# A fused routing, self-attention and cross-attention layer: the projections of each query chunk moved into the routing loop, and the last chunk's end split in two

## The reference

```python
# layer 0: routing, each 128 rows of x against all 1601 context rows
tok = input_tokens @ W_proj + b_proj
attn = softmax(prev_states @ tok.T / sqrt(D)); routed = attn @ tok
ps_n, in_n = _ln(prev_states), _ln(routed)
u, r = sigmoid([ps_n, in_n] @ W_u + b_u), sigmoid([ps_n, in_n] @ W_r + b_r)
cand = tanh([r * ps_n, in_n] @ W_n + b_n)
x = _ln((1 - u) * prev_states + u * cand)
# layer 1: 16 heads of 16
x = x + _mha(_ln(x), _ln(x), sa...)     # self-attention, 2048 keys
x = x + _mha(_ln(x), context, ca...)    # cross-attention, 1601 keys
x = x + gelu(_ln(x) @ w1.T + b1) @ w2.T + b2   # 1024 hidden
```

## Time and profile before

| what | value |
|---|---|
| median of 3 runs | 1587.95 us (1584.9 to 1590.18) |
| profiled execution | 1583.61 us, span 1581.9 us |
| PE busy | 1472.7 us, 93% of the span |
| ACT busy | 1068.4 us, 68% |
| DVE busy | 536.6 us, 34% |
| POOL busy | 43.9 us, 3% |

### The profile page before, as it was taken

How to read it: one execution, slowest core, us unless ns; L and a number is a source line. 1 busy time by engine, 2 the same in 40 slices (tenths; PEclk the granted TensorE clock), 3 DMA queues, 4 the chain that set the end, 5 groups by cost and what they waited for, 6 DMA issues and landing times.

```text
span 1581.9 us, 21204 instructions
## 1 busy us (share of the span) xinstructions
PE 1472.7 (93%) x8062; PEld 636.8 (40%) x8062; DVE 536.6 (34%) x1286; ACT 1068.4 (68%) x1285; POOL 43.9 (3%) x62
## 2 busy tenths in 40 slices
PE   8889999998787999999999999899899999999967
PEld 5467777776332222322322322222223432432334
DVE  2435555556532022232330431232332232143140
ACT  2323333332345999999999999789788787797731
POOL 2100000000110000000000000000000000000000
PEclk9999999999897999999999999899999999999988
DMA  7300000000397000010010254501000000000000
GB/s 233 153 7 7 7 7 7 7 3 0 82 245 135 18 15 11 11 49 11 12 39 22 33 94 71 113 34 34 15 19 14 22 11 11 21 15 1 8 7 14
DMA packets 37672, 64.07 MB, mean 41 GB/s; under 512 B 6164, under 2 KB 21844, under 8 KB 37428
## 3 DMA queue, kind: packets, MB, share of 16 engines
q1 hardware_dynamic: 32024, 40.87, 12.3%
q0 software_dynamic: 5552, 21.89, 3.8%
HBM read 40.85 MB, written 22.02 MB: 40 GB/s over the span
## 4 chain that ended last, share of the span: by engine, by line
PE 74%; ACT 16%; DVE 4%; issue 3%; DMA 2%; DVEq 0%; SPq 0%; ACTq 0%; POOL 0%; POOLq 0%
PE PS L962 22%; PE PS L945 16%; ACT PX L680 14%; PE PS L759 6%; PE PS L768 6%; PE PS L1019 5%; PE PS L1031 4%; PE PS L1002 2%; PE PS L805 2%; PE PS L731 2%; PE PS L706 2%; PE PS L735 1%; PE PS L777 1%; PE PS L780 1%; PE PS L981 1%
## 5 line engine op out<-in xcount | busy, mean ns | idle before, releaser
L680 ACT ACTIVATE PX<-PS 128x1024 f32<-128x1024 f32 (+1 forms) x928 | 883.9, 1039 | 144.7 <-PE PS L945 93.8
L962 PE MATMUL PS<-PX,V 128*32 128x512 f32 (+1 forms) x3712 | 500.3, 611 | 5.0 <-ACT PX L680 3.0
L945 PE MATMUL PS<-QST,stack 50*128 50x512 f32 (+1 forms) x1856 | 386.0, 473 | 24.8 <-DMA QST<-shift 10.6
L945 PEld LDWEIGHTS PS<-QST,stack 50*128 50x128 f32 (+1 forms) x1856 | 156.2, 186 | 427.4 <-ACT PX L680 341.3
L962 PEld LDWEIGHTS PS<-PX,V 128*32 128x32 f32 (+1 forms) x3712 | 73.7, 108 | 152.4 <-issue 127.1
L1381 DVE COPY OT<-PS 128x512 f32<-128x512 f32 x32 | 22.1, 692 | 302.0 <-PE PS L962 300.7
L607 ACT ACTIVATE PR<-PS,small 128x1601 f32<-128x1601 f32 x16 | 25.6, 1597 | 107.2 <-DVE small L1218 107.2
L759 PE MATMUL PS<-tokF,XT 128*128 128x512 f32 (+1 forms) x256 | 95.1, 525 | 0.6 <-DVE small L1150 0.6
L768 PE MATMUL PS<-tokT,PT 128*128 128x256 f32 (+1 forms) x416 | 93.3, 381 | 0.6 <-DVE CZ L1267 0.6
L768 PEld LDWEIGHTS PS<-tokT,PT 128*128 128x128 f32 (+1 forms) x416 | 77.9, 190 | 10.7 <-issue 0.8
L1031 PE MATMUL PS<-W,HIDT 128*128 128x256 f32 x256 | 65.2, 404 | 10.6 <-ACT HIDT L666 9.8
(11 more groups left out here) (134 smaller groups left out, 1168.4 us busy)
## 6 DMA issues: line engine op xcount, KB each, us to landing
QST<-q_parts SPq DMA_DIRECT2D x192, 64.0 KB
q_parts<-PARTS POOLq DMA_DIRECT2D x16, 512.0 KB, 5.3
stack<-k_parts SPq DMA_DIRECT2D x24, 256.0 KB, 10.1
stack<-k_parts SPq DMA_DIRECT2D x24, 200.1 KB, 6.8
k_parts<-KPARTS POOLq DMA_DIRECT2D x8, 512.0 KB, 12.6
v_cross<-V POOLq DMA_DIRECT2D x1, 3328.0 KB, 10.0
V<-v_cross SPq DMA_DIRECT2D x2, 1664.0 KB, 13.2
k_parts<-PARTS POOLq DMA_DIRECT2D x6, 512.0 KB, 3.4
```

What stands on the lines that cost most here:

```text
L680: act.activation(PX[0:kr, (2 * t + half) % 4, :, :], PS[0:kr, slot:slot + 2, :], ACT.Exp, scale=SCALE).then_inc(at["exp"], 1)
L945: ins = pe.matmul(PS[0:kr, 2 * (n % LOOK) + jj, :], KST[a][lo:lo + NROW, pair, kt * P:kt * P + kr].bitcast(F32R), QST[lo:lo + NROW, pair, ...
L962: ins = pe.matmul(PS[32 * j:32 * j + 32, 6, :], V[0:kr, kt, 2 * (g // 2 * GH + j) + g % 2, :], PX[0:kr, (2 * t + j // 2) % 4, j % 2, :], s ...
```

## The change

The routing loop is written out turn by turn on all engines. Stage 3 is cut into its four chunks. Chunk 0 comes as a whole after turn 7, chunk 1 after turn 11, chunk 3 after turn 19 (`DENSE`), and chunk 2 is put inside turns 16 and 17 (`WITHIN`), the first six entries in turn 16. In each chunk the order is now two key units, two value tiles, a query unit, the key norm, a query unit, two value tiles, the query norm. The units use banks 0 to 3, so the scores of turns 8 and 12 wait for the chunk ahead of them. The norms take these banks too, no longer bank 6. Buffers move to make room (`NQ`, `KPARTS`, `XH1`, `XHS`, `WPJ`, `CAKV`). The keys are loaded by SP for head group 0 in quarters, three of them before the drain is over, and for groups 1 to 3 whole, after the first shift rows are loaded. Queries of groups 2 and 3 come last.

The end is done in two halves of two tiles. Reciprocals read PSUM directly, the norm of two tiles is one chain on VectorE, ScalarE takes the scaling over, hidden units are 16 of 256 columns, `mlp_b2` is added to X ahead of time so that one addition a tile is left, and SP stores the last four tiles.

```diff
+END = CHUNK // 2
+END_TILES = TPC // 2
+END_HIDDEN = (0, 1, 6, 7)
+END_TURN = 4
+END_OUT = (2, 3, 4, 5)
+END_EARLY = 6
...
-        stage3 += [("q", n * CHUNK, CHUNK, mm) for mm in range(2)]
-        if n == 0:
-            stage3 += [("T", i, 0, 0) for i in range(TILES - 2, TILES)]
-        stage3 += [("k", n * CHUNK, CHUNK, 0), ("norm", CHUNKS + 2 * n, CHUNK, 0), ("k", n * CHUNK, CHUNK, 1)]
...
+        ks, qs = ([(kind, n * CHUNK, CHUNK, mm) for mm in range(2)] for kind in "kq")
+        norms = [("norm", CHUNKS + 2 * n + i, CHUNK, 0) for i in range(2)]
+        stage3.append([(10 * n + i,) + e for i, e in
+                       enumerate(ks + vs[:2] + qs[:1] + norms[:1] + qs[1:] + vs[2:] + norms[1:])])
...
+    MIDDLE = 6
+    DENSE = {2 * TPC - 1: 0, 3 * TPC - 1: 1, 5 * TPC - 1: 3}
+    WITHIN = {TILES: stage3[2][:MIDDLE], TILES + 1: stage3[2][MIDDLE:]}
...
+        def load_key_quarter(n):
+            wait_parts_stored(sp, n + 1, "k_")
+            load_keys(0, slice(n * CHUNK, (n + 1) * CHUNK), s_kst[0][n])
...
+        for i in range(2, TILES):
+            sp.wait_ge(S["l0_scores"], i - 1)
...
+            if i == 2 * TPC + 2:
+                sp.wait_ge(S["ones_copied"], 16)
+                load_ones(range(0, 2), s_kst[0][0])
+                load_key_quarter(0)
+            if i == 3 * TPC + 2:
+                load_key_quarter(1)
...
+                wait_parts_stored(sp, CHUNKS + 1)
+                for g in range(2):
+                    load_q(0, g, s_qst[0][g])
+                sp.wait_ge(S["shift_stored"], 16)
+                for g in range(2):
+                    load_shift(0, g, s_qst[0][g])
+                load_key_quarter(CHUNKS - 1)
+                for g in range(1, GROUPS):
+                    load_ones(range(2 * g, 2 * g + 2), s_kst[0][CHUNKS + g - 1])
+                    load_keys(g, slice(0, T), s_kst[0][CHUNKS + g - 1])
+                sp.wait_ge(S["shift_stored"], 16 * CHUNKS)
+                for g in range(2, GROUPS):
+                    load_q(0, g, s_qst[0][g])
...
+        for i in range(TILES - TPC, TILES):
+            sp.wait_ge(A[1]["out_ready"], i + 1)
+            sp.dma_start(out[i * P:(i + 1) * P, :], XH[:, i % TPC, :]).then_inc(S["end_stored"], 16)
...
+        def qkv(entries):
+            for u, kind, n, w, mm in entries:
+                if kind in ("k", "q"):
+                    act.wait_ge(S["qkv_unit"], done3[u])
+                    split(SQK + 4 * (n // CHUNK) + 2 * "kq".index(kind) + mm, u % 4, w, mm,
+                          col("L1_xattn_sa_b" + kind, mm))
...
+            qkv(WITHIN.get(i, ()))
...
+        for i in range(TILES + 4):
+            l0(i, i % 2, i < TILES, 1 <= i < TILES + 1, 2 <= i < TILES + 2, i >= 4)
+            if i in DENSE:
+                qkv(stage3[DENSE[i]])
...
+                def end_scaled(half):
+                    for i in range(2):
+                        act.wait_ge(at["hT"], 2 * (q + half) + i + 1)
+                        act.activation(HC[:, i, half * END:(half + 1) * END],
+                                       PS[:, END_TURN + i, half * END:(half + 1) * END], ACT.Identity,
+                                       scale=col("L1_xattn_ln3_g", i), bias=col("L1_xattn_ln3_b", i)) \
...
+                end_scaled(0)
+                act.wait_ge(at["mlp"], q * TPC)
+                for n in range(2 * units):
+                    half, i = n // units, n % units
+                    if n == END_EARLY:
+                        end_scaled(1)
+                    act.wait_ge(at["unit"], units * q + n + 1)
+                    act.activation(HIDT[:, i, half * END:(half + 1) * END],
+                                   PS[:, END_HIDDEN[n % len(END_HIDDEN)], 0:END], ACT.Gelu,
+                                   bias=col("L1_xattn_mlp_b1", i)).then_inc(at["unit_taken"], 1)
...
+        def qkv(entries):
+            for u, kind, n, w, mm in entries:
+                if u >= 4:
+                    pe.wait_ge(*taken3[u - 4])
+                if kind == "norm":
+                    norm(n, w, u % 4)
+                    continue
+                pe.wait_ge(S["ln1_taken"], (n + 1 if kind == "v" else n // P + TPC))
+                for c in range(2):
+                    if kind == "v":
+                        ins = pe.matmul(PS[:, u % 4, 0:D], hF[:, c, n * P:(n + 1) * P], SAW[:, 2, c, :],
+                                        start=(c == 0), stop=(c == 1))
+                    else:
+                        ins = pe.matmul(PS[:, u % 4, :], SAW[:, "qk".index(kind), c, mm * P:(mm + 1) * P],
+                                        hF[:, c, n:n + w], start=(c == 0), stop=(c == 1))
...
             if scores:
+                if i - 1 in DENSE:
+                    for u in range(10 * DENSE[i - 1] + 6, 10 * DENSE[i - 1] + 10):
+                        pe.wait_ge(*taken3[u])
...
+            if not gates or routed:
+                qkv(WITHIN.get(i, ()))
...
+            if gates and not routed:
+                qkv(WITHIN.get(i, ()))
...
+            def end_hidden(half, i):
+                n = half * units + i
+                if i == 0:
+                    pe.wait_ge(at["hc"], 2 * (q + 1 + half))
+                if n >= len(END_HIDDEN):
+                    pe.wait_ge(at["unit_taken"], units * q + n - len(END_HIDDEN) + 1)
+                for c in range(2):
+                    ins = pe.matmul(PS[:, END_HIDDEN[n % len(END_HIDDEN)], 0:END], W1[:, c, i * P:(i + 1) * P],
+                                    HC[:, c, half * END:(half + 1) * END], start=(c == 0), stop=(c == 1))
+                ins.then_inc(at["unit"], 1)
...
+            for half in range(2):
+                pe.wait_ge(at["normed"], CHUNKS * GP + half)
+                for i in range(half * END_TILES, (half + 1) * END_TILES):
+                    end_projection(1, i).then_inc(at["y"], 1)
+            end_turn(0)
+            for i in range(units):
+                if i == END_EARLY:
+                    end_turn(1)
+                end_hidden(0, i)
+            for i in range(units):
+                end_hidden(1, i)
+            for tt in range(TPC):
+                pe.wait_ge(at["unit_taken"], units * (q + 1 + tt // END_TILES))
+                for k in range(units):
+                    ins = pe.matmul(PS[:, END_OUT[tt], 0:D], HIDT[:, k, tt * P:(tt + 1) * P], W2[:, k, :],
+                                    start=(k == 0), stop=(k == units - 1))
+                ins.then_inc(at["mlp"], 1)
...
+                elif kind == "norm":
+                    c = (n - CHUNKS) // 2
+                    ve.wait_ge(S["norms"], n + 1)
+                    ch(ve.tensor_copy(NQ[c][:], PS[0:HEADS, u % 4, :]))
+                    ve.tensor_reduce(sm(QM + c, 1, HEADS), PS[0:HEADS, u % 4, :], AX, ALU.max) \
+                        .then_inc(S["norms_taken"], 1)
...
-            def y_tail():
+            def end():
                 q = CHUNKS - 1
-                ve.wait_ge(at["y"], (q + 1) * TPC)
+                ve.wait_ge(at["sums"], CHUNKS * GP)
+                for half in range(2):
+                    span = slice(half * END, (half + 1) * END)
+                    ch(ve.reciprocal(REC[:, span], PS[:, 7, span]))
...
+                    tiles = range(half * END_TILES, (half + 1) * END_TILES)
+                    ve.wait_ge(at["y"], q * TPC + (half + 1) * END_TILES)
...
+                    rsqrt(END_TILES, ch, i=half * END_TILES)
+                    for i in tiles:
+                        ins = ve.tensor_scalar(XH[:, i, :], X[:, q * TPC + i, :], sm(AG + 2 * i), sm(NY + i),
+                                               ALU.subtract, ALU.mult)
+                    ins.then_inc(at["hat"], 1)
...
+                    ve.wait_ge(at["mlp"], q * TPC + i + 1)
+                    ve.tensor_tensor(XH[:, i, :], PS[:, END_OUT[i], 0:D], X[:, q * TPC + i, :], ALU.add) \
+                        .then_inc(at["out_ready"], 1)
```

More of the change, by code:

```diff
@@ L981, in sums, with piece @@
                 pe.matmul(PS[:, 7, :], spread[:], SUMS[:], start=True, stop=True).then_inc(at["sums"], 1)
-            def piece(kind, i, q, part, tail=False, at=at):
-                whole = part is None
-                first, last = whole or part == 0, whole or part == PARTS_OF[kind] - 1
+            def piece(kind, i, q, part, at=at):
+                first, last = part == 0, part == PARTS_OF[kind] - 1
                 def share(n):
-                    if whole:
-                        return range(n)
                     w = n // PARTS_OF[kind]
                     return range(part * w, (part + 1) * w)
-                bank = i % 4 if tail else 7
                 if kind == "y":
@@ L1088, in _, with end_projection, end_turn @@
-            for kind, at_steps in REST[a].items():
-                for i in range(len(at_steps) // PARTS_OF[kind]):
-                    if kind != "y":
-                        piece(kind, i, CHUNKS - 1, None, True)
+            q = CHUNKS - 1
+            units = HID // P
```

(15 more changed lines are left out.)

299 lines of the change are left out of this document (114 added, 185 removed).

## The result

The changed kernel takes 1572.84 us in the median of four runs (1571.22 to 1573.64), against 1587.87 us for the kernel before in its four runs (1584.9 to 1590.18). The ratio is 0.9913, with a 95% interval from 0.9896 to 0.9931: 13.8 us faster, between 11.0 and 16.5 (the two medians alone lie 15.0 us apart). The forecast was 8.0 us faster, 1580.0 us, in a range from 1571 to 1589.

What follows compares the result with a forecast made beforehand. PE was taken to bound the routing loop (busy 38.2 of 40 us), with chains of waits after it and at the end. Head +0.3 and end -8.3 gave -8.0 us: median 1580.0 us, eight-in-ten range 1571 to 1589.

Steps and rivals of the forecast that it cites:

- the likeliest case: The forecast itself: whole kernel net -12 to -4.7 us, 1576 to 1583 us; chance 0.45.
- Part 6: End after attention: output 7.0 us earlier by halves, 1.3 from one add less and SP for POOL; sum -8.3.
- Part 1: Chunks 0 and 1 inside the routing loop: 18.0 us a chunk with seams, 36.0 for two.
- Written-out loop: Routing loop: writing it out removes PE idle time at six back edges, at most 0.7 us.
- Part 2: Chunk 2 inside turns 16 and 17: adds 16.5 us, with candidate matmuls at half clock.
- Part 3: Chunk 3 waits for tile 15 in hF after turn 17, PE having nothing to do: 12.9 us.
- Part 4: From tile 15 in hF to self-attention's first score: 23.7 us, or 31 if the shift's store is slow.
- Part 5: Self-attention keys loaded in pieces: enough cover for each load, so it costs nothing.
- Seams hidden: Loop and drain: chunks cost only PE's 13.8 us in the loop, head gains 8, 1572 us; chance 0.15.
- The head eats the gain: Head: slow shift store (+7) or seams 2 to 3 us more each, end still gives 8, 1586 us; chance 0.25.
- Half clock at every seam: Around chunks 0 and 1: PE falls to 1.2 GHz, costing 13.8 us, 1594 us; chance 0.15 with its like.

Runs made afterwards that it cites:

- e3: Kernel before, with only the last four tiles' stores moved from POOL to SP: 1578.53 us, ratio 0.9951.
- e4: Changed kernel, with POOL storing the last four tiles again: 1576.29 us, ratio 0.9936.
- e5: Changed kernel, with chunks 0 and 1 one turn later and the next turn's scores waiting bank by bank: 1566.51 us, ratio 0.9873.
- e10: Changed kernel without the branch on the first flag (self-attention), and shift rows stored ahead of the last query part: 1569.28 us, ratio 0.9908.
- e1: Kernel before, with only the new end (two halves, last four stores on SP): 1573.24 us, ratio 0.9917.
- e7: Changed kernel, with POOL storing the first shift rows ahead of the last query part: 1571.2 us, ratio 0.9907.
- e6: Changed kernel, with chunks 0 to 2 back to back after turn 17 and key quarters loaded behind XT: 1561.97 us, ratio 0.9858.
- e2: Changed kernel with the old end, POOL storing: 1586.91 us, ratio 1.001.

## Why the prediction was right, and where it was not

The direction and the range held, and most steps of the head and of the end's computation did. The forecast was short by 5.8 us by the ratio, and nearly all of that is one term. That the time fell inside the range was in part luck: it lies 1.8 us above its lower end, outside the 1576 to 1583 that the likeliest case alone was given. The range reached so far down for the rival of hidden seams, and that is not what came.

**The term that was mis-sized: Part 6, SP in place of POOL and one addition less, -1.3 us.** It measured -6.3 us (8.9 to 2.6 behind the last matmul). The prediction compared issue and landing on the two queues, and took the rest up to the end of the span as the same for both. What it left out was POOL's DRAIN, 4.73 us, which starts only when POOL's last store has landed. e3 and e4 give -5.6 and +5.7 us for the queue alone. With -6.3 in place of -1.3 the sum is -13.0 us and the median 1575.0; it measured 13.8 us less by the ratio. The Trainium skill's figures ("DMA: Bandwidth & Descriptors", "Latency and other measured facts", 0.6 against 1 us to the first byte) would have given 0.4 us for the queue; the 0.9 to 1.0 us that remain in e3 and e4 beside the DRAIN are of that kind, but over twice as large. The Trainium skill ("VectorE: DVE Perf Modes", "The DRAIN you can't avoid") tells of DRAINs of about 12 ns on all five engines from the runtime's preamble and postamble. The rows here carry a line of the program itself, so they may be others; SP's 13 ns are near that figure, and POOL's 4402 to 4728 ns are not.

**Part 6, the rest: right.** Hidden units 6.8 us earlier were forecast, 6.9 came; the end of the output 7.0, and 7.3 came. The two halves of hidden units run without a gap (7.93, 0.44, 8.63 us), and the GELUs and the second half's scaling are hidden.

**Part 1, 18.0 us a chunk in the loop: 18.4 measured, so 0.8 us more for two.** Both seams are there as described. e5 shows what lies in them: 3.8 us a chunk, near the lower bound of 13.8 us that PE's work alone would need (14.6 measured).

**Written-out loop, -0.7 us:** up to turn 15's scores the head is 35.1 us later than before (389.78 against 354.65), with 36.8 us for two chunks, so -1.7. Only 1.05 us of it came in turns 4 to 15, where a turn takes 20.03 instead of some 20.14 us; the other 0.65 us was there at turn 4's scores already (132.42 against 133.07 us), and both kernels have turns 0 to 3 written out.

**Part 2, chunk 2 in turns 16 and 17, +16.5 us: 15.2 measured** (CZ of turn 17 at 451.73 us, forecast near 453). The half clock came in turn 16 (granted clock 0.58 from 433.3 to 437.0 us) but not fully in turn 17 (1.00 until 450.0 us, then 0.52 until 452.0):

```profile
433.35 2.08 PE L877 MATMUL PS<-W,RPS 128*128 128x256 f32 x4 [4.11 <-DVE RPS L1361]
...
448.93 1.13 PE L877 MATMUL PS<-W,RPS 128*128 128x256 f32 x4 [2.73 <-DVE RPS L1361]
449.90 1.72 PE L877 MATMUL PS<-W,CF 128*128 128x256 f32 x4
```

After 4.11 us of idle PE the first four of the eight matmuls took 2.08 us. After 2.73 us they took 1.13, which is what the same four take in a steady turn, and only the next four were slow (1.72, against 1.02 in a steady turn). The prediction had 3.8 us for all eight here and 2.70 came. That is not a property of the gap. In e5, behind the same gap in the same turn, all eight ran at full speed, and so they did in e10:

```profile
440.37 1.13 PE L877 MATMUL PS<-W,RPS 128*128 128x256 f32 x4 [2.73 <-DVE RPS L1361]
441.34 1.03 PE L877 MATMUL PS<-W,CF 128*128 128x256 f32 x4
```

**Part 3, 12.9 us for tile 15: 12.75 measured** (451.73 to 464.48).

**Part 4, 23.7 us from hF to the first score: 26.2 measured.** The shift rows were ready after 17.5 us (forecast 16.9) and their store began after 19.5 (18.95). It landed in 3.00 us (2.7). The load and first matmul took 3.7 in place of 2.0 us, and 1.7 of that is the branch. "Keys first" is what put it there: before, the norm of the last queries was taken ahead of the last key norm, and the flag stood at 479.3 us, 10.2 ahead of the first score. Now the query norm is the last entry of the chunk and the flag stands at 485.9 us, 4.8 ahead. The prediction moved the query norm and did not ask who waits for it: its "load and first matmul, 2.0 us" has no term for the branch. Part 4 was 2.5 us too low and Part 1 0.8, and Part 2 (1.3), the loop and its start (1.0) and Part 3 (0.15) made up for all but 0.9 us of that. That the first score was forecast to within 1 us is these misses cancelling.

**Part 5, keys in pieces, nothing:** no wait for the stack appears; attention took 1031.8 us against 1030.6. The kernel before, e1 and e3 have the same code up to the end of attention and took 1030.6, 1027.3 and 1033.5 us, so a difference of 1.2 us can't be told from none.

**The rivals.** *Seams hidden* had the time nearly right (1572) and was wrong: the seams were not hidden, and the gain came from the end. e5 shows what it would have brought. *The head eats the gain* did not come: the slow landing of 9.9 us did not return (3.00, 2.20 and 3.03 us in the changed kernel, e7 and e6). *Half clock at every seam* did not come: the eight matmuls behind a gap of 1.66 us took 3.70 us, against 3.60 with no gap in e5 (both by the timeline), and the scores behind the other seam 5.78 against 5.74. The granted clock of that stretch is 1.00, the 2.4 GHz level. The Trainium skill ("TensorE: Matmul & The Clock Gate", section on HAM oscillation) has bursts of matmuls start cold behind DMA waits of about 3 to 5 us. That section does not speak of gaps as short as 1.7 us, which cost nothing here; at 4.1 us the trace agrees with it.

## What to carry to other kernels

Ask who issues the last DMA and look at what each engine's sequencer does after it: the time behind the last landing is not fixed, and moving four stores off GpSimd was worth 5.6 us here, nearly as much as all the rework of the last chunk's arithmetic (7.3). A piece of work that is put into a busy pipeline costs its own length plus its seams, so place it where its inputs are long ready and let what follows wait buffer by buffer, or put such pieces end to end (e5 and e6: 6 and 9 us on top of the change). When an entry changes its place in an order, ask for every semaphore that it raises who waits there, the control flow too.

## What was not expected of the hardware

- GpSimd's closing DRAIN took 4.73 us in the three kernels where it stores the last four tiles (before, e2, e4) and 4.40 us in the others, each time beginning 2.2 us after the issue of its last store, which takes 2.0 to land. No run here has it without a store just ahead, and what it does in that time is open. TensorE's took 4.07 us and VectorE's up to 466 ns, but these end within 0.06 us of the engine's last instruction (17 ns where VectorE had nothing running); SyncE's took 13 to 294 ns. None of these shows in the page or in the chain of waits.
- From a flag written by VectorE to the first matmul behind TensorE's branch on it, 4.8 to 6.9 us passed in four kernels; the branch instruction alone was 3.56 to 5.65 us of it, and 7.35 us in the kernel before, where it was hidden.
- Idle PE of 1.66 us did not lower the speed of the next matmuls, 4.11 us slowed all of the next eight (the first four 2.08 against 1.13). Behind the same 2.73 us the second four took 1.57 to 1.72 us in five kernels and 1.03 in two (e5, e10), so the gap's length alone does not decide. After some 11 us with a few transposes the next eight of 512 columns took 5.07 to 6.72 us in different kernels, against 3.63 without a gap.
